# Where a softmax is divided by its sums: values normalised as they leave PSUM, or in the stage behind

## The chip, the cores and the metric

The kernel runs on one core of a Trainium2 chip. The metric is device time in microseconds (us) of a whole execution; lower is better. TensorE (PE in the profile) multiplies matrices into PSUM, VectorE (DVE) and ScalarE (ACT) read PSUM, GpSimd (POOL) works in SBUF, SyncE (SP) issues most transfers.

## The reference, cut to what matters

Two transformer layers with adaptive normalisation and experts. Only the first attention is touched: two softmaxes per head, whose difference is weighted with a number per head, lambda, and then normalised by its root mean square.

```python
lam = exp(sum(lambda_q1 * lambda_k1, -1)) - exp(sum(lambda_q2 * lambda_k2, -1)) + 0.8
A1, A2 = Q1 @ K1^T / sqrt(16), Q2 @ K2^T / sqrt(16)        # causal
attn = softmax(A1) - lam * softmax(A2)                     # B=2, H=16, N=2048
O = attn @ V                                               # 32 columns a head
O = O / sqrt(mean(O * O, -1) + 1e-5) * rms_scale * 0.2
x = x + gate * (O @ W_o^T)
```

## The kernel before, in words

`program` runs stages one after the other; a stage ends when all its engines have ended. `attention0` is the first attention, `attention0_out` (named `out0` in its buffers) the stage behind it.

**attention0** loops over 32 heads (batch times head). A head has 40 steps (`STEPS`), one for each pair of a query tile of 512 and a key block of 128 that the causal mask leaves; query tile 0 ends at step 3, tile 1 at 11, tile 2 at 23, tile 3 at 39 (`LAST`). Two steps make one iteration of TensorE. In an iteration TensorE computes four scores (L743, with the mask in L747) into a ring of three `ps_s`, ScalarE takes their exponentials into `probs` (L665), TensorE multiplies them with the values (L772) for both softmaxes at once, POOL adds the probabilities of the two steps (L635), and TensorE sums those over the keys with a matrix of ones (L783). Values and sums of a query tile lie in one `ps_o`, of which there are two: `[:, 0]` holds values, `[:, 1]` the sums, already repeated over the 32 rows of each value.

Between these matmuls TensorE slips in the *maxima* of a later head: 80 matmuls a head (L793) into a ring of three `ps_m`, of which VectorE takes the row maximum, with the mask (L691, two instructions) or without (L695). `maxima_at` spreads them: 42 in steps 20 to 39 for the head after the next one, and the other 38 in steps 0 to 17 for the next head. TensorE waits before each for `max_used`, that is until VectorE has read the maximum three before. After the 80th, VectorE reduces them (L699), TensorE turns them, VectorE splits them into three bf16 parts (L707 to L710) and SP writes those into the next head's `q_stack` (L598). For the first head all 80 of its own maxima come before its scores, and the next head's 80 are all in its steps 0 to 17.

When a query tile has ended, ScalarE copies values and sums, 512 columns, from `ps_o` to `results` (`take`, L650). `ends(k, 5)` puts that five steps after the tile's last step: before the exponentials of steps 8, 16 and 28 and of step 4 of the next head. It waits for the last ones matmul of the tile, and TensorE waits for `taken` before it starts the tile after next. SP then stores values (L613) and sums (L615), in two halves each, to `heads_out` and `exp_sums` in DRAM.

**attention0_out** works in 8 groups of 512 tokens, each in four tiles. SP loads `heads` and `total` of a group. TensorE turns the sums (L1048) and the heads (`turn`, L1056) so that tokens are rows. VectorE inverts the sums and weights the second one with lambda (L995, L997), multiplies (`normalise`, L1003), POOL subtracts (L951) and squares (L954), VectorE adds up the squares (L981). For the group before, meanwhile, `norm` takes L985, ScalarE's root, the reciprocal L987 and L990; TensorE turns back (L1063) and multiplies with W_o (L1086), and VectorE gates (L1011) and adds to x (L1014). In a step VectorE does `norm(now)`, the inversion, `normalise(after, 0)`, and then for each tile j `normalise(after, j + 1)`, `add(now, j)` and the squares of j. The stage begins with nine small loads (L903 to L907, four of them the lambdas) and the computation of lambda on VectorE and ScalarE.

The order around the takes, before:

```python
for k in range(N_STEPS):
    for a in range(2):
        ended = ends(k, 5)
        if a == 0 and ended and not (ended[1] and is_first(head)):
            take(head - 1 if ended[1] else head, ended[0])
```

## Time and profile before

| | us |
|---|---|
| three runs, median | 4081.42 (4077.68 to 4083.18) |
| the profiled execution, its own time | 4081.09 |
| its span, first to last instruction | 4079.1 |
| VectorE busy in the span | 2409.2 (59%) |
| ScalarE busy | 1599.8 (39%) |
| POOL busy | 1706.1 (42%) |

Durations come from the one profiled execution, whose time is 2.0 us above its span. In the list of groups a row gives line, engine, operation, output and input tiles, their shapes and the count; then the time in which the group was busy and the mean of one in ns; then how long the engine was idle just before and what ended that. In the order of time a row gives start and duration in us; several instructions of one kind may be merged into one row.

### The profile page before, as it was taken

Reading aid. Unit: us, or ns where it says so; the run is one execution under the profiler, and the core shown is the slowest. Engines: PE = TensorE matmul, PEld = TensorE weight load, DVE = VectorE, ACT = ScalarE, POOL = GpSimd, SP = SyncE. Lnnn points to the kernel's source line nnn. Section 1 sums busy time; section 2 is a strip of 40 time slices with the busy share of each in tenths; the row PEclk is TensorE's granted clock in tenths of the full one; section 3 lists DMA queues with packets and bytes.
Section 4 is the critical chain, followed back from the end, with each engine's and each line's share of the span. In section 5 each row is a group of like instructions: output and inputs, shape, how many; then the busy total and the mean of one; then the engine's idle time right before and its main releaser. Section 6 shows DMA issues by size and latency. Waiting matters only on the chain. (4 is left out here: it accounts for less than half of the span.)

```text
span 4079.1 us, 84288 instructions
## 1 busy us (share of the span) xinstructions
PE 3494.4 (86%) x27311; PEld 1870.2 (46%) x27311; DVE 2409.2 (59%) x5524; ACT 1599.8 (39%) x3266; POOL 1706.1 (42%) x1117
## 2 busy tenths in 40 slices
PE   6868999999999999999999967527999579895993
PEld 3322444444444444444444446524555345554562
DVE  3448777777777777777777347673111666666013
ACT  2322666666666666666666621101221321111110
POOL 1221665655656566656566644002443231110203
PEclk8987999999999999999999978557999789995997
DMA  4441111111111111111111031104332100001333
GB/s 156 145 141 41 35 42 43 35 46 42 34 46 36 41 42 35 47 36 41 44 35 46 11 119 65 43 0 119 78 80 52 43 15 0 1 0 50 115 113 93
DMA packets 229279, 224.88 MB, mean 55 GB/s; under 512 B 88722, under 2 KB 198547, under 8 KB 222739
## 3 DMA queue, kind: packets, MB, share of 16 engines
q1 hardware_dynamic: 213522, 194.33, 16.1%
q0 software_dynamic: 15360, 25.44, 3.2%
q8 instruction: 227, 3.72, 0.4%
q14 instruction: 170, 1.38, 0.1%
HBM read 138.58 MB, written 80.35 MB: 54 GB/s over the span
## 5 line engine op out<-in xcount | busy, mean ns | idle before, releaser
L635 POOL TENSOR_TENSOR attention_probs<-attention_probs 128x1024 f32<-128x1024 f32 (+2 forms) x640 | 1228.8, 1920 | 868.6 <-PE attention_ps_o L772 868.6
L665 ACT ACTIVATE attention_probs<-attention_ps_s 128x512 f32<-128x512 f32 (+3 forms) x2560 | 1197.7, 538 | 838.2 <-PE attention_ps_s L747 466.1
L695 DVE TENSOR_REDUCE attention_chunk_max<-attention_ps_m 128x1 f32<-128x512 f32 x1536 | 1005.5, 686 | 247.4 <-PE attention_ps_m L793 245.3
L793 PE MATMUL attention_ps_m<-attention_k_stack,attention_q_stack 96*128 96x512 bf16 (+3 forms) x2560 | 878.4, 358 | 43.2 <-DMA attention_v_head<-v_rows 33.9
L743 PE MATMUL attention_ps_s<-attention_q_stack,attention_k_stack 99*128 99x512 bf16 (+3 forms) x2560 | 798.5, 351 | 40.3 <-issue 27.2
L772 PE MATMUL attention_ps_o<-attention_probs,attention_v_head 128*32 128x256 f32 (+1 forms) x9728 | 640.5, 366 | 0.7 <-ACT attention_probs L665 0.4
L691 DVE CUSTOM_DVE_ANT_0 attention_ps_m<-attention_ps_m,attention_mask_wide 128x128 f32<-128x128 f32 (+3 forms) x1024 | 500.2, 498 | 219.3 <-PE attention_ps_m L793 201.7
L793 PEld LDWEIGHTS attention_ps_m<-attention_k_stack,attention_q_stack 96*128 96x128 bf16 x2560 | 243.6, 97 | 458.4 <-DVE attention_chunk_max L695 184.0
L783 PE MATMUL attention_ps_o<-attention_probs,consts 128*32 128x256 f32 (+1 forms) x5120 | 415.5, 360 | 0.4 <-POOL attention_probs L635 0.4
L772 PEld LDWEIGHTS attention_ps_o<-attention_probs,attention_v_head 128*32 128x32 f32 x9728 | 264.4, 109 | 273.6 <-issue 111.2
L743 PEld LDWEIGHTS attention_ps_s<-attention_q_stack,attention_k_stack 99*128 99x128 bf16 x2560 | 247.5, 98 | 306.1 <-ACT attention_probs L665 144.7
L783 PEld LDWEIGHTS attention_ps_o<-attention_probs,consts 128*32 128x32 f32 x5120 | 189.3, 110 | 89.5 <-POOL attention_probs L635 14.2
L747 PE MATMUL attention_ps_s<-mask_k_bf,ident_bf 128*128 128x128 bf16 x1024 | 221.4, 222 | 0.0
L1574 DVE TENSOR_TENSOR experts_hidT<-experts_ps_b,experts_silu 128x512 f32<-128x512 f32 x64 | 44.2, 691 | 238.4 <-ACT experts_silu L1540 238.4
L1521 POOL DMA_INDIRECT experts_sum<-experts_y_sb,experts_index x64 | 100.7, 1574 | 144.5 <-ACT experts_y_sb L1548 129.9
L379 POOL TENSOR_TENSOR project_parts<-project_rest,project_parts 128x512 bf16<-128x512 f32 x64 | 73.6, 1156 | 198.5 <-ACT project_parts L364 198.5
L2224 DVE TENSOR_SCALAR experts_hidT<-experts_ps_a 128x512 f32<-128x512 f32 x32 | 22.1, 691 | 212.3 <-PE experts_ps_a L2242 212.3
L691 DVE DVE_READ_ACCUMULATOR2_ANT attention_chunk_max<- 128x1 f32 x1024 | 144.9, 142 | 0.0
L1860 POOL TENSOR_TENSOR x<-x,linear_y 128x256 f32 (+1 forms) x32 | 24.6, 769 | 275.3 <-DVE linear_y L1918 275.3
L1957 PE MATMUL linear_ps_a<-linear_qblk,linear_kc 128*128 128x512 f32 x256 | 125.2, 616 | 3.2 <-POOL linear_vp L1856 2.7
L439 PE MATMUL project_ps_o<-project_hT,project_wqkv 128*128 128x512 f32 x256 | 113.4, 601 | 13.0 <-ACT project_hT L353 13.0
L1610 PE MATMUL experts_ps_y<-experts_w,experts_hidT 128*128 128x256 f32 x512 | 114.7, 382 | 10.4 <-DVE experts_hidT L1574 10.4
(278 smaller groups left out, 3935.2 us busy)
## 6 DMA issues: line engine op xcount, KB each, us to landing
qk_parts<-project_parts SPq DMA_DIRECT2D x64, 384.0 KB, 3.0
heads_out<-attention_results_sb SPq DMA_DIRECT2D x256, 64.0 KB
out_heads<-heads_out SPq DMA_DIRECT2D x8, 2048.0 KB, 7.9
experts_w<-in_f_w SPq DMA_DIRECT2D x16, 1024.0 KB, 8.4
attention_q_stack<-qk_parts SPq DMA_DIRECT2D x32, 384.0 KB
attention_k_stack<-qk_parts SPq DMA_DIRECT2D x32, 384.0 KB
experts_w<-in_e_w SPq DMA_DIRECT2D x24, 512.0 KB, 4.7
v_rows<-project_v SPq DMA_DIRECT2D x8, 1024.0 KB, 4.0
```

The source lines that it names most:

```text
L439: last = pe.matmul(ps_o[o % RING][:], w[:, o // 4, k, (o % 4) * P:(o % 4 + 1) * P], hT[:, k], start=(k == 0), stop=(k == DC - 1))
L635: pool.tensor_tensor(probs[:, to, :, lo:], probs[:, to, :, lo:], probs[:, k % RING_P, :, lo:], ALU.add).then_inc(pair_ok, 1)
L665: act.activation(probs[:, k % RING_P, a, left(k):], ps_s[(2 * k + a) % RING_S][:, left(k):], ACT.Exp, scale=float(DH) ** -0.5).then_inc(pr ...
L691: last = dve.tensor_tensor_reduce(ps_m[m % RING_M][:, 0:w], ps_m[m % RING_M][:, 0:w], mask_wide[:, GROUP - w:], 1.0, -3.0e38, ALU.add, ALU ...
L695: last = dve.tensor_reduce(to, ps_m[m % RING_M][:, 0:w], AX.X, ALU.max)
L743: last = pe.matmul(psum[:, lo:], ks[at][0:WITH_MAX, a, kb * P:(kb + 1) * P], qs[at][0:WITH_MAX, a, tq * GROUP + lo:(tq + 1) * GROUP], star ...
L747: last = pe.matmul(psum[:, lo:lo + P], core.ident_bf[:], core.mask_k_bf[:], start=False, stop=True)
L772: last = pe.matmul(psum[strip:strip + DV, 0, block:], vh[at][:, kb], halves(k, a, half, block), start=kb == 0, stop=False, tile_position=( ...
L783: last = pe.matmul(psum[strip:strip + DV, 1, block:], core.c("ones")[:, 0:DV], halves(k, a, half, block), start=False, stop=kb == GT * (tq ...
L793: pe.matmul(ps_m[m % RING_M][:, 0:w], qs[at][0:STACK, a, jq * P:(jq + 1) * P], ks[at][0:STACK, a, c * GROUP:c * GROUP + w], start=True, st ...
L1610: last = pe.matmul(ps_y[n][:, c], hT[:, m, (2 * n + c) * P:(2 * n + c + 1) * P], w_down[now.at][:, m], start=(m == 0), stop=(m == MC - 1))
L1957: last = pe.matmul(ps_a[hg][:, 4 * n:4 * n + 4].rearrange("p h t -> p (h t)"), kc[1 - at][:, hg], qblk[:, hg, 4 * n:4 * n + 4].rearrange(" ...
```

## The change

The division moves forward. In `attention0`, VectorE and no longer ScalarE takes a finished tile: a reciprocal of the 256 columns of sums from PSUM to SBUF, then one `scalar_tensor_tensor` that multiplies the 256 columns of values with a factor per partition and with the inverse. The factor is 1 on the partitions of the first softmax and minus lambda on those of the second. It is computed once, by VectorE and ScalarE, after the first head's maxima (`factors`), and its four loads are issued after the first head's. The take comes three steps after the tile's end (before the maxima of steps 6, 14, 26 and of step 2 of the next head). `results` has half its columns, and only values are stored. In `attention0_out` the totals, their transposes and their inversion go; ScalarE copies the second softmax's part from PSUM (`second`), VectorE adds the first one's to it (`difference`), and POOL only squares. The lambdas' loads and their computation are gone from the stage's start.

The diff, cut to its core:

```diff
@@ -44,7 +44,8 @@
...
                       ("iota", P), ("part", 1), ("headof", NE), ("blockdiag", NE * 17), ("tile_of", T * NE),
-                      ("expert", NE), ("expert_base", NE)):
+                      ("expert", NE), ("expert_base", NE),
+                      ("first_map", 1), ("second_map", 1)):
     CONSTS[_name] = (_at, _at + _width)
@@ -72,6 +73,8 @@
...
     put("expert_base", np.arange(NE)[None, :] * CAP1)
+    put("first_map", p // DV % 2 == 0)
+    put("second_map", -(p // DV % 2.0))
     return c
@@ -504,7 +507,11 @@
...
         probs = s.sb("probs", [P, RING_P, 2, GROUP], F32)
-        results = s.sb("results_sb", [P, RING_R, 2, BLOCKS, P], F32)
+        results = s.sb("results_sb", [P, RING_R, BLOCKS, P], F32)
+        inverse = s.sb("inverse_sb", [P, 2, BLOCKS, P], F32)
+        lam_in = s.sb("lam_in", [P, 4, H, DH], F32)
+        lam_two = s.sb("lam_two", [P, 2, H], F32)
+        factor = s.sb("factor", [P, B, H], F32)
         mask_wide = s.sb("mask_wide", [P, GROUP], F32)
@@ -583,6 +590,9 @@
...
                     load(after)
+                    for n, a in enumerate(lambdas):
+                        sp.dma_start(lam_in[:, n], a.rearrange("h d -> (h d)").partition_broadcast(P)
+                                     .rearrange("p (h d) -> p h d", h=H)).then_inc(lam_loaded, 16)
                 if later is not None:
@@ -611,10 +621,7 @@
...
                     sp.dma_start(oT[ds(h, 1), :, tile * GROUP:(tile + 1) * GROUP].rearrange(
-                        "n e (u v t) -> v (n e) u t", v=2, t=P)[half], results[rows, slot, 0]).then_inc(stored[slot], 16)
-                    sp.dma_start(sums[ds(h, 1), :, tile * GROUP:(tile + 1) * GROUP].rearrange(
-                        "n e (u v t) -> v (n e) u t", v=2, t=P)[half],
-                        results[half * 2 * DV:(half + 1) * 2 * DV:DV, slot, 1]).then_inc(stored[slot], 16)
+                        "n e (u v t) -> v (n e) u t", v=2, t=P)[half], results[rows, slot]).then_inc(stored[slot], 16)
@@ -640,14 +647,8 @@
...
-            act.sem_inc(taken, RING_O)
-            def take(head, turn):
-                slot = turn % RING_R
-                act.wait_ge(stored[slot], (head * (Q_TILES // RING_R) + 1) * (STORES * 16))
-                act.wait_ge(values_ok, head * N_STEPS + LAST[turn] + 1)
-                act.wait_ge(ones_ok, head * PAIRS + (LAST[turn] + 1) // PAIR + RING_P // PAIR)
-                act.activation(results[:, slot], ps_o[turn % RING_O][:], ACT.Copy).then_inc(taken, 1)
+            act.wait_ge(lam_steps, 3)
+            act.activation(lam_two[:], lam_two[:], ACT.Exp).then_inc(lam_exp, 1)
@@ -655,17 +656,12 @@
...
                     for a in range(2):
-                        ended = ends(k, 5)
-                        if a == 0 and ended and not (ended[1] and is_first(head)):
-                            take(head - 1 if ended[1] else head, ended[0])
                         act.wait_ge(score_ok, head * 2 * N_STEPS + 2 * k + a + 1)
...
                                        ACT.Exp, scale=float(DH) ** -0.5).then_inc(prob_ok, 1)
-                if after is None:
-                    take(head, Q_TILES - 1)
@@ -680,7 +676,34 @@
             dve.sem_inc(max_used, RING_M)
+            dve.sem_inc(taken, RING_O)
             dve.wait_ge(ready, 1)
+            def factors():
+                link = Counted(dve, lam_steps)
+                dve.wait_ge(lam_loaded, 4 * 16)
+                link.then(dve.tensor_tensor(lam_in[:, 0], lam_in[:, 0], lam_in[:, 1], ALU.mult))
+                link.then(dve.tensor_tensor(lam_in[:, 2], lam_in[:, 2], lam_in[:, 3], ALU.mult))
+                dve.tensor_reduce(lam_two[:, 0], lam_in[:, 0], AX.X, ALU.add)
+                link.then(dve.tensor_reduce(lam_two[:, 1], lam_in[:, 2], AX.X, ALU.add))
+                dve.wait_ge(lam_exp, 1)
+                link.then(dve.tensor_tensor(factor[:, 0], lam_two[:, 0], lam_two[:, 1], ALU.subtract))
+                link.then(dve.tensor_scalar(factor[:, 0], factor[:, 0], LAMBDA_INIT, core.c("second_map"), ALU.add,
+                                            ALU.mult))
+                link.then(dve.tensor_scalar(factor[:, 0], factor[:, 0], core.c("first_map"), None, ALU.add))
+                link.then(dve.tensor_copy(factor[:, 1], factor[:, 0]))
+            def take(head, turn):
+                psum, slot = ps_o[turn % RING_O], turn % RING_R
+                wait_apart(dve, values_ok, head * N_STEPS + LAST[turn] + 1, core.passed)
+                dve.wait_ge(ones_ok, head * PAIRS + (LAST[turn] + 1) // PAIR + RING_P // PAIR)
+                dve.reciprocal(inverse[:, turn % 2], psum[:, 1]).then_inc(inverted, 1)
+                wait_apart(dve, stored[slot], (head * (Q_TILES // RING_R) + 1) * (STORES * 16), core.passed)
+                dve.wait_ge(inverted, head * Q_TILES + turn + 1)
+                dve.scalar_tensor_tensor(results[:, slot], psum[:, 0],
+                                         factor[:].rearrange("p b h -> p (b h)")[:, ds(head, 1)],
+                                         inverse[:, turn % 2], ALU.mult, ALU.mult).then_inc(taken, 1)
@@ -714,11 +737,17 @@
...
                     maxima(next_head.n, range(len(MAXIMA)))
+                    factors()
                     return
                 for k in range(N_STEPS):
+                    ended = ends(k, 3)
+                    if ended and not (ended[1] and is_first(at_head.n)):
+                        take(at_head.n - 1 if ended[1] else at_head.n, ended[0])
                     whose, items = maxima_at(at_head.n, k, next_head, later)
...
                         maxima(whose.n, items)
+                if next_head is None:
+                    take(at_head.n, Q_TILES - 1)
@@ -913,31 +933,35 @@
...
                     "(r n) e t -> (n e) r t", n=2)).then_inc(loaded[at], 16)
-                sp.dma_start(total[at][:], sums[b * H:(b + 1) * H, :, ds(start, GROUP)].rearrange(
-                    "n e t -> (n e) t")).then_inc(loaded[at], 16)
...
                         step(b, i * 2 + (b * NG + at), i, at)
-            sp.wait_ge(loaded[0], B * NG * 16)
-            sp.wait_ge(loaded[1], B * NG * 16)
+            sp.wait_ge(loaded[0], B * NG // 2 * 16)
+            sp.wait_ge(loaded[1], B * NG // 2 * 16)
...
         def _(act):
-            act.wait_ge(lam_prod, 1)
-            act.activation(lam_two[:], lam_two[:], ACT.Exp).then_inc(lam_exp, 1)
+            def second(after, j):
+                act.wait_ge(turned_h, after * GT + j + 2 + GT)
+                act.wait_ge(sum_ok, after * GT + j + 1)
+                act.activation(two[:, j % 2], ps_h[j % 2][:, :, 1], ACT.Copy).then_inc(two_ok, 1)
             def step(now, after, at, pair):
-                if now is None:
-                    return
-                act.wait_ge(mean_ok, now + 1)
-                act.activation(mean[at][:], mean[at][:], ACT.Sqrt).then_inc(root_ok, 1)
+                if now is not None:
+                    act.wait_ge(mean_ok, now + 1)
+                    act.activation(mean[at][:], mean[at][:], ACT.Sqrt).then_inc(root_ok, 1)
+                if after is not None:
+                    second(after, 0)
                 for j in range(GT):
-                    act.wait_ge(y_ok, now * GT + j + 1)
-                    act.wait_ge(turned_o, now * GT + j + 1)
-                    act.activation(oT_sb[:, j % 2], ps_t[:], ACT.Copy).then_inc(oT_ok, 1)
+                    if after is not None and j + 1 < GT:
+                        second(after, j + 1)
+                    if now is not None:
+                        act.wait_ge(y_ok, now * GT + j + 1)
+                        act.wait_ge(turned_o, now * GT + j + 1)
+                        act.activation(oT_sb[:, j % 2], ps_t[:], ACT.Copy).then_inc(oT_ok, 1)
@@ -947,33 +971,22 @@
...
                 for j in range(GT):
-                    pool.wait_ge(two_ok, after * GT + j + 3)
-                    pool.tensor_tensor(o[1 - at][:, j], two[:, j, :, 0], two[:, j, :, 1], ALU.subtract)\
-                        .then_inc(sub_ok, 1)
-                    pool.wait_ge(sub_ok, after * GT + j + 1)
+                    pool.wait_ge(sum_ok, after * GT + j + 3)
                     pool.tensor_tensor(square[:, j], o[1 - at][:, j], o[1 - at][:, j], ALU.mult).then_inc(square_ok, 1)
         def _(dve):
-            chain = Counted(dve, lam_ok)
-            dve.wait_ge(w_in, 16 * 9)
-            chain.then(dve.tensor_tensor(lam_in[:, 0], lam_in[:, 0], lam_in[:, 1], ALU.mult))
-            chain.then(dve.tensor_tensor(lam_in[:, 2], lam_in[:, 2], lam_in[:, 3], ALU.mult))
-            dve.tensor_reduce(lam_two[:, 0], lam_in[:, 0], AX.X, ALU.add)
-            dve.tensor_reduce(lam_two[:, 1], lam_in[:, 2], AX.X, ALU.add).then_inc(lam_prod, 1)
-            dve.wait_ge(lam_exp, 1)
-            chain.then(dve.tensor_tensor(lam[:], lam_two[:, 0], lam_two[:, 1], ALU.subtract))
-            chain.then(dve.tensor_scalar(lam[:], lam[:], LAMBDA_INIT, None, ALU.add))
+            chain = Counted(dve, gate_ok)
+            dve.wait_ge(w_in, 16 * 5)
             dve.tensor_scalar(w[:].rearrange("p k n -> p (k n)"), w[:].rearrange("p k n -> p (k n)"), scale[:, 0:1],
...
-            dve.sem_inc(two_ok, 2)
+            dve.sem_inc(sum_ok, 2)
             dve.sem_inc(x_ok, 4)
@@ -990,20 +1003,9 @@
...
-            def invert_totals(after):
-                dve.wait_ge(turned_l, after + 1)
-                dve.reciprocal(recip[:], ps_l[:]).then_inc(l_steps, 1)
-                dve.wait_ge(l_steps, 2 * after + 1)
-                dve.tensor_tensor(recip[:, :, :, 1], recip[:, :, :, 1],
-                                  lam[:].unsqueeze(1).broadcast_to([P, GT, H]), ALU.mult).then_inc(l_steps, 1)
-                dve.wait_ge(l_steps, 2 * after + 2)
-            def normalise(after, j):
-                dve.wait_ge(turned_h, after * GT + j + 2 + GT)
-                dve.tensor_tensor(two[:, j].rearrange("p h a d -> p (h a) d"),
-                                  ps_h[j % 2][:].rearrange("p h a d -> p (h a) d"),
-                                  recip[:, j].rearrange("p h a -> p (h a)").unsqueeze(2)
-                                  .broadcast_to([P, 2 * H, DV]), ALU.mult).then_inc(two_ok, 1)
+            def difference(after, j, at):
+                dve.wait_ge(two_ok, after * GT + j + 1)
+                dve.tensor_tensor(o[at][:, j], ps_h[j % 2][:, :, 0], two[:, j % 2], ALU.add).then_inc(sum_ok, 1)
@@ -1018,12 +1020,11 @@
...
                 if after is not None:
-                    invert_totals(after)
-                    normalise(after, 0)
+                    difference(after, 0, 1 - at)
                 for j in range(GT):
                     if after is not None and j + 1 < GT:
-                        normalise(after, j + 1)
+                        difference(after, j + 1, 1 - at)
                     if now is not None:
@@ -1040,18 +1041,9 @@
-            def turn_totals(after, place, pair):
-                wait_apart(pe, loaded[place], pair * 32 + 32, core.passed)
-                for j in range(GT):
-                    last = pe.matmul(ps_l[:, j].rearrange("p h a -> p (h a)"), total[place][:, j * P:(j + 1) * P],
-                                     core.c("ident")[0:2 * H, 0:2 * H], start=True, stop=True)
-                last.then_inc(turned_l, 1)
             def turn(after, place, j):
-                pe.wait_ge(two_ok, after * GT + j + 1)
+                pe.wait_ge(sum_ok, after * GT + j + 1)
                 for r in range(ROWS):
@@ -1066,7 +1058,7 @@
                 if after is not None:
-                    turn_totals(after, 1 - at, pair + at)
+                    wait_apart(pe, loaded[1 - at], (pair + at) * 16 + 16, core.passed)
                     turn(after, 1 - at, 0)
```

## Rows read from the trace of the kernel before

**Rows 1.** Stretch: us; PE, PEld, DVE, ACT, POOL busy; PEclk, DMA share, GB/s

```profile
380.00:2373.00 1993.00, 1949.84 (x20793) 908.48 (x20791) 1422.60 (x3581) 1237.73 (x2667) 1221.77 (x637) 0.99 0.15 38
```

**Rows 2.** Instructions of the line that ends each head's maxima

```profile
L699 DVE TENSOR_REDUCE attention_neg_max<-attention_chunk_max x32: 285/286/289, 352.1 to 2289.5; 128x32 f32<-128x128 f32 x32
```

**Rows 3.** Instruction groups by form: busy us, mean ns, idle before

```profile
L650 ACT ACTIVATE attention_results_sb<-attention_ps_o 128x512 f32<-128x512 f32 x128 | 75.9, 593 | 2.1 <-PE attention_ps_o L783 2.1
L987 DVE RECIPROCAL out_mean_sq<-out_mean_sq 128x64 f32<-128x64 f32 x8 | 4.4, 553 | 2.6 <-ACT out_mean_sq L935 2.6
L995 DVE RECIPROCAL out_recip<-out_ps_l 128x128 f32<-128x128 f32 x8 | 7.6, 950 | 4.5 <-PE out_ps_l L1048 4.5
L1189 DVE SCALAR_TENSOR_TENSOR gates_h<-gates_scaled,gates_rstd,rows 128x256 f32<-128x256 f32 x64 | 26.8, 480 | 3.4 <-DVE gates_scaled L1182 3.4
```

**Rows 4.** VectorE in order of time, in one head: start us, duration us

```profile
1236.73 1.28 DVE L695 TENSOR_REDUCE attention_chunk_max<-attention_ps_m 128x1 f32<-128x512 f32 x2
...
1261.50 0.69 DVE L695 TENSOR_REDUCE attention_chunk_max<-attention_ps_m 128x1 f32<-128x512 f32 x1
...
1267.42 0.29 DVE L691 CUSTOM_DVE_ANT_0 attention_ps_m<-attention_ps_m,attention_mask_wide 128x128 f32<-128x128 f32 x1
...
1279.90 0.42 DVE L691 CUSTOM_DVE_ANT_0 attention_ps_m<-attention_ps_m,attention_mask_wide 128x256 f32<-128x256 f32 x1
1280.24 0.69 DVE L695 TENSOR_REDUCE attention_chunk_max<-attention_ps_m 128x1 f32<-128x512 f32 x1
1281.96 1.29 DVE L695 TENSOR_REDUCE attention_chunk_max<-attention_ps_m 128x1 f32<-128x512 f32 x2 [1.03 <-PE attention_ps_m L793]
```

**Rows 5.** TensorE in the same stretches

```profile
1238.65 0.38 PE L793 MATMUL attention_ps_m<-attention_k_stack,attention_q_stack 96*128 96x512 bf16 x1
...
1263.18 0.33 PE L793 MATMUL attention_ps_m<-attention_k_stack,attention_q_stack 96*128 96x384 bf16 x1
...
1270.39 0.38 PE L793 MATMUL attention_ps_m<-attention_k_stack,attention_q_stack 96*128 96x512 bf16 x1
...
1281.98 0.38 PE L793 MATMUL attention_ps_m<-attention_k_stack,attention_q_stack 96*128 96x512 bf16 x1
...
1283.06 0.38 PE L793 MATMUL attention_ps_m<-attention_k_stack,attention_q_stack 96*128 96x512 bf16 x1
```

**Rows 6.** Order of time, VectorE after the first head's maxima

```profile
360.59 0.30 DVE L691 CUSTOM_DVE_ANT_0 attention_ps_m<-attention_ps_m,attention_mask_wide 128x128 f32<-128x128 f32 x1 [6.47 <-PE attention_ps_m L793]
```

**Rows 7.** One line of the stage behind, once a group

```profile
L985 DVE TENSOR_SCALAR out_mean_sq<-out_mean_sq x8: 194/195/196, 2406.8 to 2554.7; 128x64 f32<-128x64 f32 x8
```

**Rows 8.** Order of time in the stage behind, VectorE and POOL

```profile
2445.18 0.41 DVE L1011 TENSOR_TENSOR out_gated<-out_ps_y,out_gate 128x256 f32<-128x256 f32 x1
2445.34 1.26 POOL L951 TENSOR_TENSOR out_o<-out_two 128x512 f32<-128x512 f32 x1 [0.91 <-DVE out_two L1003]
2445.74 1.14 DVE L1014 TENSOR_TENSOR x<-x,out_gated 128x256 f32 x1
...
2452.53 0.95 DVE L995 RECIPROCAL out_recip<-out_ps_l 128x128 f32<-128x128 f32 x1
...
2453.86 1.23 DVE L1003 TENSOR_TENSOR out_two<-out_ps_h,out_recip 128x1024 f32<-128x1024 f32 x1
```

**Rows 9.** A group by form: an addition-like instruction of PSUM and SBUF

```profile
L1574 DVE TENSOR_TENSOR experts_hidT<-experts_ps_b,experts_silu 128x512 f32<-128x512 f32 x64 | 44.2, 691 | 238.4 <-ACT experts_silu L1540 238.4
```

**Rows 10.** Order of time, start of the stage behind

```profile
2376.87 0.37 SPq L903 DMA_DIRECT2D out_lam_in<-in_lq  x1
...
2378.71 0.43 SPq L905 DMA_DIRECT2D out_wo<-in_wo  x1
...
2391.48 1.88 PE L1048 MATMUL out_ps_l<-consts,out_total 32*128 32x32 f32 x8 [20.93 <-DMA out_total<-exp_sums]
```

**Rows 11.** Stretches again, for the granted clock (columns as in rows 1)

```profile
1005.00:1006.00 1.00, 0.72 (x5) 0.50 (x6) 0.00 (x0) 0.08 (x1) 0.00 (x0) 0.50 0.63 188
...
2425.00:2430.00 5.00, 3.04 (x25) 2.69 (x24) 4.47 (x9) 0.26 (x1) 1.90 (x2) 1.00 0.36 128
```

More of the change, by code:

```diff
@@ L487, in __init__, with attention0 @@
         self.n, self.at, self.round = STACKS * i + n, n % STACKS, i + n // STACKS
-def attention0(nc, core, qk_parts, v_rows, oT, sums):
+def attention0(nc, core, qk_parts, v_rows, oT, lambdas):
     with stage(nc, "attention0") as s:
@@ L524, in attention0 @@
         PAIRS = N_STEPS // PAIR
[L525 removed]
+        STORES = 2
         LAST = [k for k, (_, tq, kb) in enumerate(STEPS) if kb == GT * (tq + 1) - 1]
@@ L868, in attention0_out @@
         heads = [s.sb(f"heads{i}", [P, 2 * DQ // P, GROUP], F32) for i in range(2)]
-        total = [s.sb(f"total{i}", [2 * H, GROUP], F32) for i in range(2)]
-        recip = s.sb("recip", [P, GT, H, 2], F32)
-        two = s.sb("two", [P, GT, H, 2, DV], F32)
+        two = s.sb("two", [P, 2, H, DV], F32)
         o = [s.sb(f"o{i}", [P, GT, H, DV], F32) for i in range(2)]
@@ L901, in _ @@
         def _(sp):
-            for n, a in enumerate(lambdas):
-                sp.dma_start(lam_in[:, n], a.rearrange("h d -> (h d)").partition_broadcast(P)
-                             .rearrange("p (h d) -> p h d", h=H)).then_inc(w_in, 16)
             sp.dma_start(w[:], woT.rearrange("(k p) n -> p k n", p=P)).then_inc(w_in, 16)
```

24 lines of the change are left out of this document (9 added, 15 removed).

## The prediction

> **What bounds the kernel now.** I read the stage windows first, to see which engine fills the first attention. There TensorE is busy 1949.84 of 1993 us, VectorE 1422.60, ScalarE 1237.73, at a granted clock of 0.99, that is 2.4 GHz [rows 1]. In VectorE's order of time the pauses end with TensorE's matmuls L793, as the 1.03 us before 1281.96 [rows 4]: it has idle time and TensorE has none. The line that closes each head's maxima (L699) starts 32 times, from 352.1 to 2289.5 us, so a head takes 62.5 us on average [rows 2]. Whatever holds TensorE there counts in full, 32 times over; whatever VectorE gets counts only where its idle time and the three ps_m buffers don't cover it. The stage behind alternates: VectorE works alone on norm and totals while TensorE waits, then both work.
>
> **What leaves ScalarE.** 128 copies of 0.593 us, 75.9 us in all [rows 3]. ScalarE idles 755 us of the stage and TensorE's iterations with such a copy are no longer than those without, so I take 0; in the last one and a half heads, where no maxima fill TensorE, five copies may be worth up to 0.5 us each: -1 us of the -2.5 to 0.
>
> **What comes to VectorE.** 128 takes: a reciprocal of 256 columns out of PSUM and a scalar_tensor_tensor of 256 columns. Reciprocals of 64 and 128 columns took 553 and 950 ns [rows 3]: 6.2 ns a column, so 950 + 128 x 6.2 = 1744 ns for 256. The nearest scalar_tensor_tensor took 480 ns [rows 3], and its successor can start some 80 ns before its end, as successive maxima do (1279.90 + 0.42 against 1280.24 [rows 4]). With 0.04 us for the wait between the two, a take holds VectorE for 1.74 + 0.04 + 0.40 = 2.18 us. The Trainium skill ("VectorE: DVE Perf Modes", First, the fixed hardware budget) states that Reciprocal is an iterative divide with a repeat count of 8; at the page's 0.96 GHz that would be 8.3 ns a column, an estimate of 2.0 us for 256 and a sum some 33 us higher. The rows show 6.2 ns, and the sum goes by them.
>
> Where does it hit? VectorE meets a take before the maxima of steps 2, 6, 14 and 26 of the 40. The ones matmuls that it needs are over by then, since TensorE has already issued the maxima of the two steps before, so the take itself waits for nothing. But the next maximum starts 2.18 us later, and TensorE may be only three maxima ahead. For step 14 of one head: VectorE would start the next maximum not at 1279.90 but at 1282.08 and end it at 1282.50 [rows 4]. TensorE's matmul of 1281.98 writes that buffer again [rows 5]; with 0.05 us for the semaphore it starts at 1282.55, 0.57 late. The next maxima follow at 1282.42 and 1283.02 and the third ends at 1283.71; the matmul of 1283.06, late by 0.57, is held until 1283.76: 0.70 us lost. VectorE then catches up in the 1.03 us in which it idled [rows 4]. In the same way step 2 (VectorE 1261.50, TensorE's matmul of 1263.18): 1261.50 + 2.18 + 0.69 + 0.05 = 1264.42, 1.24 late. Step 26 (1236.73 and 1238.65): 1239.65, 1.00 late. Step 6 (1267.42 and 1270.39): the maxima of 0.21 and 0.60 go first, the third ends at 1271.10, so 1271.15, 0.76 late [rows 4, 5]. Together 3.70 us a head. TensorE has nothing to catch up with, so they stay.
>
> 30 takes of each of the four kinds fall beside maxima: 30 x 3.70 = 111 us. The two of the first head fall where 80 maxima are crowded into 18 steps and VectorE is nearly the bound: 2 us each, 4 us. The other six have no maxima behind them; the last one ends the stage with 2.18 instead of 0.59 us, and two DMA issues of L615 drop out, an estimated 0.6 us each: +0.4 us. Waits that could replace it: values of the turn after next need the buffer that a take frees; the nearest is step 2, over at 1261.50 + 2.18 = 1263.68, and needed by values that follow two more maxima behind the matmul of 1263.18 [rows 5], still in time. SP's stores come two steps earlier, half as many. The lambdas' chain, eight small instructions and one of ScalarE, falls into the gap of 6.47 us in which VectorE waits before the second head's maxima [rows 6]: 0, and if the chain did not fit, 3 us at most. **Attention: +114 us**, bounds +66 (each take 0.4 us cheaper, as small gaps ahead of TensorE's values absorb some) and +155 (0.3 us dearer, if register work ahead of each wait shows, and 4 more).
>
> **The stage behind.** The eight L985 start from 2406.8 to 2554.7, 21.1 us apart [rows 7]. After norm, VectorE inverts the totals from 2452.53 to 2453.86 and then normalises in 1.22 us, after which TensorE may go on [rows 8]. That becomes one addition of PSUM and SBUF of 512 columns, 0.69 us as L1574 [rows 9]; ScalarE copies its part (about 0.59 us, as L650 [rows 3]) while VectorE norms. Saved: 1.33 + 0.53 = 1.86 us. Behind it VectorE has two more normalisations on its path: 2 x 0.53 = 1.06. So 2.9 us in each of 7 cycles: 20.3 us. At the start: four lambda loads issued before the rest, 2376.87 to 2378.71, 1.84 us; the transposed totals, 1.88 us [rows 10]; 1.3 us in the first tile (copy and addition for normalisation and POOL's difference), and about 0.8 us in each of three tiles whose pace POOL sets, with 1.26 us for the difference [rows 8] ahead of the square: 7.4 us. **Stage behind: -28 us**, bounds -38 (the shorter pause leaves TensorE at 2.4 GHz) and -10 (only the inversion counts).
>
> Sum: 111 + 4 - 1 + 0.4 - 27.7 = +87 us, on the profiled execution's own 4081.09 us, which is 0.3 us below the median of the three runs: 4168 us.
>
> **The rivals.**
> *Absorbed, so faster.* The takes would vanish in VectorE's idle time. Idle time is enough on average (570 us against 279), which speaks for it; against it, the idle pieces are about 1 us long and a take 2.18. The lost 3.70 us a head are 4 x 2.18 less a cover of 5.0, 1.25 us a take, so net zero needs 0.22 us lost, a take of about 1.5 us. That wants a reciprocal nearer to 1 us; the rows would have to bend. With no loss at all it gives 4081 - 28 = 4053 us. Chance of landing below -0.2%: 0.06, and 0.03 between.
> *POOL's sums block the new instruction.* An addition with both inputs in SBUF (L1014) took 1.14 us while POOL's L951 ran, though it is as wide as L1011 just before it; L1011, with one input in PSUM, kept its 0.41 beside the same POOL instruction [rows 8]. The new instruction has one tensor in PSUM, one in SBUF and a pointer scalar in SBUF. If it is held like L1014, POOL's sums, busy 1221.77 of 1993 us [rows 1], cost 0.61 x about 1.1 = 0.7 us a take: + 85, 4253 us. 0.07. The Trainium skill ("SBUF — State Buffer", Who interferes with whom) states that VectorE with two SBUF inputs contends with a GpSimd instruction that reads SBUF, and with one at most it does not; whether the scalar counts decides this rival. For plain tensors the rows agree.
> *The clock falls.* After a pause of 3.7 us in TensorE the granted clock was 0.50, that is 1.2 GHz [rows 11]. If each 1 us hole did that for some 5 us, half of it lost, 122 x 2.5 = 305: 4473 us. Against it: 3.04 busy of 5 us left it at 1.00 [rows 11]. 0.03. The Trainium skill ("TensorE: Matmul & The Clock Gate", A second HAM failure mode) tells of a kernel where short idles between groups made the clock oscillate; by it this rival would be the forecast.
> *No cover at all.* VectorE the bound, each take in full: 122 x 2.18 - 28: 4319 us. 0.03.
>
> **The numbers.** Forecast 0.78; the rest as above. From the bounds: 4081 + 66 - 38 = 4109 and 4081 + 155 - 10 = 4226; widened by a us or two the range is 4108 to 4228, with the rivals outside it. What a measurement can tell here is about 0.2%, 8 us. Slower 0.91, same 0.03, faster 0.06.
>
> **What would show it.** Reciprocal rows near 1744 ns and the other near 480, x128; VectorE near 1700 us busy in the stage; heads 3.7 us longer each; TensorE's waits for VectorE grown by some 110 us, clock still 0.99; L985 about 18.2 us apart. Wrong if heads keep their length, or if scalar_tensor_tensor rows spread up to 2 us.

## The result and the profile after

The changed kernel takes 4175.53 us (median of 4 runs, 4173.57 to 4180.96) against 4082.30 us before: ratio 1.0231, 95% interval 1.0216 to 1.0245, so 93 us slower. The forecast was 4168, +87. The profiled execution took 4175.89 us, its span 4174.1; that is 95.0 us above the span before. By stages of the two traces: first attention (end of the first head's maxima to the issue of the last store, which before is one of the sums) 2148.7 against 2021.7 us, +127.0 (forecast +114); the stage behind it, to its last addition to x, 165.9 against 196.4, -30.5 (forecast -28); all else -1.5.

The page's first part, and the stretch that answers to [rows 1] (the attention now ends near 2500):

```profile
PE 3511.1 (84%) x27247; PEld 1863.0 (45%) x27247; DVE 2634.2 (63%) x5766; ACT 1572.2 (38%) x3170; POOL 1663.1 (40%) x1085
380.00:2500.00 2120.00, 1985.55 (x20815) 913.58 (x20807) 1678.07 (x3839) 1194.49 (x2541) 1222.69 (x637) 0.99 0.14 35
```

TensorE is busy for 94% of the stretch where it was 98%. Its idle time went from 43 to 134 us; its busy time too is 36 us longer, for as many matmuls. VectorE has 255 us more work and 442 us left idle. The granted clock is again 0.99. The two new groups, and the line that closes each head's maxima [rows 2], then the one of the stage behind [rows 7]:

```profile
L701 DVE RECIPROCAL attention_inverse_sb<-attention_ps_o 128x256 f32<-128x256 f32 x128 | 224.1, 1751 | 67.8 <-PE attention_ps_o L812 67.2
L704 DVE SCALAR_TENSOR_TENSOR attention_results_sb<-attention_ps_o,attention_factor,attention_inverse_sb 128x256 f32<-128x256 f32 x128 | 61.9, 484 | 8.0
L722 DVE TENSOR_REDUCE attention_neg_max<-attention_chunk_max x32: 285/286/289, 352.5 to 2416.4; 128x32 f32<-128x128 f32 x32
L998 DVE TENSOR_SCALAR out_mean_sq<-out_mean_sq x8: 194/194/195, 2525.2 to 2652.7; 128x64 f32<-128x64 f32 x8
```

The reciprocal took 1751 ns (forecast 1744), the multiplication 484 (480). A regular head, from one L722 to the next, is 65.0 to 65.2 us instead of 61.2: +3.9 (forecast 3.70). The groups of the stage behind stand (2652.7 - 2525.2) / 7 = 18.2 us apart, as forecast.

Step 14 of one head in order of time, VectorE and TensorE; it answers to [rows 4, 5], and it is the place that the prediction worked out:

```profile
1279.53 1.75 DVE L701 RECIPROCAL attention_inverse_sb<-attention_ps_o 128x256 f32<-128x256 f32 x1
1281.17 0.39 PE L822 MATMUL attention_ps_m<-attention_k_stack,attention_q_stack 96*128 96x512 bf16 x1
1281.32 0.48 DVE L704 SCALAR_TENSOR_TENSOR attention_results_sb<-attention_ps_o,attention_factor,attention_inverse_sb 128x256 f32<-128x256 f32 x1
1281.72 0.42 DVE L714 CUSTOM_DVE_ANT_0 attention_ps_m<-attention_ps_m,attention_mask_wide 128x256 f32<-128x256 f32 x1
1282.25 0.39 PE L822 MATMUL attention_ps_m<-attention_k_stack,attention_q_stack 96*128 96x512 bf16 x1 [0.48 <-DVE attention_chunk_max L714]
```

From the start of the take to the next maximum it is 1281.72 - 1279.53 = 2.19 us (forecast 2.18); then TensorE sits for 0.48 us until a maximum has freed its buffer. Summed over the stretch, the waits (us in total, times, longest; of the loading of weights, PEld, and of the matmuls, PE):

```profile
PEld attention_ps_m L822 <- DVE attention_chunk_max L718: 266.2, 587, 2.7
PEld attention_ps_m L822 <- DVE attention_chunk_max L714: 116.9, 254, 1.0
PE attention_ps_m L822 <- DVE attention_chunk_max L718: 60.3, 65, 2.4
PE attention_ps_m L822 <- DVE attention_chunk_max L714: 28.3, 64, 0.7
```

The second pair was 1.9 and 1.3 us before. It grew to 88.6 us over 129 waits: one real pause of the matmuls for each take. It is less than the 127.0 us lost. The ends of matmuls are modelled in this profile, so that part of each stall may stand in it as busy time, the 36 us above; that is argued and not shown.

The first head lost 7.5 us (64.2 against 56.7). In order of time, and the granted clock behind it (stretches, last three columns clock, DMA share, GB/s):

```profile
378.78 0.39 PE L822 MATMUL attention_ps_m<-attention_k_stack,attention_q_stack 96*128 96x512 bf16 x1 [2.39 <-DVE attention_chunk_max L718]
379.10 1.67 PE L801 MATMUL attention_ps_o<-attention_probs,attention_v_head 128*32 128x256 f32 x16
...
380.00:382.00 2.00, 2.00 (x18) 0.60 (x11) 0.13 (x1) 0.00 (x0) 1.13 (x1) 0.50 0.13 45
```

There the maxima are crowded, the pause was 2.39 us, and the clock fell to 0.50, that is 1.2 GHz: the 16 matmuls of values took 1.67 us, where they took 1.07 just before. The second take of that head did the same. After the pauses of the regular takes, 0.8 to 1.3 us, it did not fall.

### The profile page after: what moved, and what is told of

It is laid out like the page before. It is cut to its first block and busy times, and to the rows that moved or that the text cites. A ratio compares the mean times of both kernels' runs of the same rounds, so it can differ in the third digit from the quotient of the medians.

```text
span 4174.1 us, 83875 instructions
## 1 busy us (share of the span) xinstructions
PE 3511.1 (84%) x27247; PEld 1863.0 (45%) x27247; DVE 2634.2 (63%) x5766; ACT 1572.2 (38%) x3170; POOL 1663.1 (40%) x1085
## 5 line engine op out<-in xcount | busy, mean ns | idle before, releaser
L701 DVE RECIPROCAL attention_inverse_sb<-attention_ps_o 128x256 f32<-128x256 f32 x128 | 224.1, 1751 | 67.8 <-PE attention_ps_o L812 67.2
```

What stands on the lines that cost most here:

```text
L701: dve.reciprocal(inverse[:, turn % 2], psum[:, 1]).then_inc(inverted, 1)
```

## The experiments

The theory: TensorE has work in stock for about 1 to 1.5 us of VectorE's absence, the *cover*; what a take lasts beyond it is lost, and VectorE's idle total is of no account. Below, *excess* is how much longer an iteration of TensorE (two steps) is than in the first experiment, by the distance of ScalarE's exponentials four apart in the trace, as the median over heads. It is given for the take or piece that causes it; where the table of experiment 6 names steps, they are those of the exponentials, and what VectorE does at one step shows there two steps later.

**1. No reciprocal.** Take of 0.48 us; the division is left out, a constant 1 stands in its place.

```diff
+dve.memset(inverse[:], 1.0)
...
-dve.reciprocal(inverse[:, turn % 2], psum[:, 1]).then_inc(inverted, 1)
+dve.sem_inc(inverted, 1)
```

> The changed kernel without the attention's reciprocals: the values are multiplied by a constant 1 where the inverse of the sums stood, so the division is left out. Everything else, the wait for the sums at VectorE included, stands as in the changed kernel. Theory (the length of the take beyond what TensorE's stored work covers, 0.94 to 1.48 us by position, is what costs): a take of 0.48 us is covered at all four positions, a regular head falls from 65.0 to 61.2 us as before, the attention from 2148.7 to about 2022 us, and with the faster out stage (166 us) the total is about 4050 us. Rival (the wait for the sums at the front of VectorE's queue holds back the maxima, whatever the length of the take): the wait stays, so the heads stay between 63 and 65 us and the total lies between 4110 and 4175 us.

Measured: 4051.23 us (6 runs), ratio 0.993 (0.9909 to 0.9951). Regular head 61.1 to 61.2 us, attention 2026.6 (before: 2021.7), stage behind 166.1. The wait for the sums still stands in front of VectorE's queue and costs nothing in a regular head: there the length of the reciprocal is the whole loss. The attention is still 4.9 us longer than before: 1.5 us in the first head, 4.6 us in the eight heads in which the loop turns (one in three), less 1.1 us behind the last maxima. This kernel has no reciprocal, so none of that is the reciprocal's.

**2. ScalarE takes the values alone.** VectorE takes nothing; division and lambda are left out.

```diff
+act.activation(results[:, slot], ps_o[turn % RING_O][:, 0], ACT.Copy).then_inc(taken, 1)
```

> ScalarE takes the turns as in the kernel before and at its place, but only the 256 columns of the values; VectorE takes nothing. The division and the weighting with lambda are left out; the out stage is the changed one. Theory: ScalarE's copies of half the size cost TensorE nothing, a regular head is 61.2 us, the attention is within 2 us of 2021 us, the out stage 166 us, and the total about 4050 us, within 5 us of the kernel without reciprocals. Rival (taking the copies off ScalarE was worth something that the gain of the kernel without reciprocals includes): the heads here are 0.3 to 1 us longer than in that kernel, and the total is 10 to 30 us above it.

Measured: 4054.06 us (4 runs), ratio 0.9934 (0.9909 to 0.9959); regular head 61.2, attention 2027.1. That ScalarE is relieved is worth nothing that can be seen, as the prediction had it. Both kernels show about what the new stage behind is worth: -29 to -32 us by the medians.

**3. More beyond the cover.** A second reciprocal of 256 columns, and in another kernel one of 128, written to a tile that nobody reads.

```diff
+dve.reciprocal(again[:], psum[:, 1])
 dve.reciprocal(inverse[:, turn % 2], psum[:, 1]).then_inc(inverted, 1)
```

> The changed kernel with each of the attention's reciprocals run twice, the first into a tile that nobody reads. Theory (the cover is used up, so that each further microsecond of VectorE at a take is a microsecond of TensorE): 1.75 us more a take, the four iterations of a head with a take lengthen by 2.5 to 3.0 us over before, a head is 72 us, and the total is 4175.5 + 128 x 1.75 = about 4400 us. Rival (pauses of TensorE as long as the 2.39 us one of the first head halve the granted clock each time): each take costs 2 to 3 us more again, a head is 80 us or more, and the total is 4650 us or more, with granted clock 0.50 behind each take. Second rival (VectorE has 570 us of idle time in the steady stretch before and takes up work without loss): less than 4300 us.

> The changed kernel with a further reciprocal of 128 columns at each take, into a tile that nobody reads: half of what the kernel with two reciprocals adds. It gives a point between pauses of TensorE of 1 us, behind which the granted clock stayed at 1.00, and the 2.4 us pause of the first head, behind which it fell to 0.50. Theory (linear while the clock holds): 0.95 us more a take, 3.8 us a head, 69 us a head, total 4175.5 + 128 x 0.95 = about 4297 us, and the granted clock stays at 1.00 in regular heads. Rival (the clock already falls at pauses near 2 us): some heads 71 us and more with stretches at 0.50, total 4330 us or more.

Measured: 4533.34 us with 256 columns more, between the theory's 4400 and the rival's 4650; 4346.10 with 128 more, where the theory gave 4297 and its rival, that the clock falls, 4330 or more: there the rival holds (two runs each). In stretches of clock 1.00 the theory is nearly right: at step 14 the excess went from 0.65 us to 1.46 (of 0.95 us added) and 2.26 (of 1.75 added), 0.85 to 0.92 us for each microsecond. The rest is the clock. The smaller dose, TensorE in order of time and the stretches from 966 us:

```profile
966.12 0.34 PE L824 MATMUL attention_ps_m<-attention_k_stack,attention_q_stack 96*128 96x384 bf16 x1 [1.89 <-DVE attention_chunk_max L720]
966.29 0.85 PE L774 MATMUL attention_ps_s<-attention_q_stack,attention_k_stack 99*128 99x512 bf16 x2
966.94 0.63 PE L824 MATMUL attention_ps_m<-attention_k_stack,attention_q_stack 96*128 96x512 bf16 x1
...
966.00:970.00 4.00, 3.88 (x25) 1.51 (x28) 2.99 (x9) 1.68 (x3) 0.00 (x0) 0.57 0.19 63
970.00:973.00 3.00, 3.00 (x39) 1.54 (x35) 2.26 (x4) 2.04 (x4) 2.35 (x1) 1.00 0.19 71
```

The matmul that took 0.39 us takes 0.63. Such a fall made an iteration 4.91 us instead of 3.33, so 1.6 us each, and came one, two or three times a head (heads of 69.7, 71.3 and 72.8 us; with none, an estimate from these, it would be about 68.2); over 380 to 2350 us the granted clock was 0.95, with the full second reciprocal 0.91. Pauses of 1.2 to 2.7 us were followed by a fall at some times and not at others.

**4. The take at another place.** The same take two steps later.

```diff
-ended = ends(k, 3)
+ended = ends(k, 5)
```

> The changed kernel with each whole take five steps behind the turn's end, where ScalarE took it before, and not three. Nothing else differs. Theory (TensorE's cover differs by position, and at step 4 it is the bank itself that TensorE waits for): the turns 0, 1 and 2 cost 0.7 to 1.3 us each, turn 3 about 3.4 us, 1.3 of maxima and 2 of waiting for its bank at the next head's turn 1; a regular head is 66.5 to 67.5 us and the total 4220 to 4260 us. Rival (the place is of no account, only the length is): 65 us a head and 4175 us.

Measured: 4274.25 us (2 runs), above both the theory's 4260 and the rival's 4175. A regular head is 68.0 to 68.7 us in twenty cases and 66.5, as the theory had it, in two. In these two the excess by take is 2.0 us for the one at step 4, 1.26 at step 8, 1.11 at step 16 and 0.97 at step 28. So the place counts. At step 4 it is the bank of the turn after next that is not free; in the waits of TensorE, from 380 us:

```profile
PE attention_ps_o L801 <- DVE attention_results_sb L704: 55.0, 28, 2.0
```

That is 1.96 us in each of 28 heads, a wait that the changed kernel does not have. It stands in place of the stall for the maxima there and is not added to it, as the expectation had it (1.3 and 2).

The other 1.6 us of a head are the clock again. In 27 of the 30 heads with maxima it fell behind this very pause. The matmuls behind it in two heads one after the other, and the stretches (the last three columns are clock, DMA share, GB/s):

```profile
533.57 1.07 PE L801 MATMUL attention_ps_o<-attention_probs,attention_v_head 128*32 128x256 f32 x16 [1.93 <-DVE attention_results_sb L704]
600.10 1.94 PE L801 MATMUL attention_ps_o<-attention_probs,attention_v_head 128*32 128x256 f32 x16 [1.93 <-DVE attention_results_sb L704]
...
533.50:536.50 3.00, 2.94 (x35) 1.55 (x35) 2.56 (x7) 1.07 (x3) 1.75 (x1) 1.00 0.19 66
600.00:603.00 3.00, 2.90 (x26) 1.27 (x27) 1.31 (x4) 0.00 (x0) 0.85 (x1) 0.51 0.19 66
```

Both pauses are 1.93 us; behind the first the clock stays at 1.00 and the 16 matmuls take 1.07 us, behind the second it is 0.51 and they take 1.94. Of the 3.1 us by which a head of 68.1 is longer than the changed kernel's 65.0, the place has 1.5 and the clock 1.6.

**5. The take in pieces.** The whole computation; the reciprocal in two halves, at iterations of their own.

```diff
+dve.reciprocal(inverse[:, turn % 2, u], psum[:, 1, u]).then_inc(inverted, 1)   # u = 0, 1
...
+OFFSETS = ((3, 3, 3, 3), (5, 5, 5, 5), (5, 5, 5, 5))    # halves: steps behind the end, by turn
+OFFSETS = ((3, 3, 3, 3), (5, 5, 5, 3), (7, 7, 7, 3))    # thirds
```

> The whole computation of the changed kernel, with the take in two parts: the reciprocal of the first 128 columns of the sums at three steps behind the turn's end (0.95 us by the row of that size), the one of the other 128 and the multiplication two steps later (0.95 + 0.48 us). VectorE's work is the same plus 0.15 us a take. Theory (a cover for each iteration, 0.94 to 1.48 us): the first part is hidden everywhere, the second exceeds the cover by 0 to 0.5 us at a take; a regular head is 61.2 to 63 us and the total 4050 to 4110 us, 4070 the likeliest. Rival (the cover is a stock that is used up once and is not filled again two steps later, or it is VectorE's total that counts): the heads stay at 65 us or above and the total at 4175 us or above.

> The whole computation, the take in three parts for turns 0, 1 and 2: the reciprocal of the first 128 columns of the sums three steps behind the turn's end, the one of the other 128 five steps, the multiplication seven steps behind; the turn 3 is taken whole at three steps behind, as in the changed kernel. Theory (a piece of up to about 1 us is covered and the cover is full again two steps later, and the take in halves lost most of what it lost because TensorE waited at the turn 1's first values for the turn 3's bank, 82 us, 2.2 us a head of 63.4): the turns 0, 1 and 2 cost nothing, turn 3 costs its 1.3 us as in the changed kernel, a regular head is 62.5 us, the total 4050 + 32 x 1.3 = about 4092 us. Rival (the sum of VectorE's work near a turn's end counts, however it is cut): 63.4 us or more a head and 4132 us or more, since a further instruction is added.

Halves: 4132.40 us, ratio 1.0129 (1.0101 to 1.0157), regular head 63.4: below the rival's 4175, but above the theory's 4110 and 63 us. Thirds: 4102.87 us, 1.0045 (1.0029 to 1.0061), 62.5. So the cover is there anew at each iteration: the first halves of 0.95 us cost 0 everywhere, though VectorE's work grew. The second part of 1.43 us cost 0.46, 0.31 and 0.17 us at steps 8, 16 and 28, and 1.28 us at step 4. The expectation for the thirds put 2.2 us a head on that last wait; this added PEld's and PE's waits, which lie mostly in the same time, and PE's alone are 1.24 us each, near the 1.28 of the excess (the waits of the halves' kernel):

```profile
PEld attention_ps_o L819 <- DVE attention_results_sb L708: 44.9, 27, 1.7
PE attention_ps_o L819 <- DVE attention_results_sb L708: 37.1, 30, 1.3
```

That bank wait is what the halves' expectation had left out. The thirds' head of 62.5 us was right: turns 0, 1 and 2 at 0, turn 3, still taken whole at step 2, at 1.23. The total was forecast as 4092, 11 us too low; the regular heads are not where that was missed.

**6. ScalarE empties PSUM, VectorE divides the copy.** Full computation. ScalarE copies 512 columns at five steps as before; VectorE's pieces follow from SBUF, where no bank waits for them.

```diff
+act.activation(raw[:, turn % 2], ps_o[turn % RING_O][:], ACT.Copy).then_inc(taken, 1)
...
+dve.reciprocal(inverse[:, turn % 2, u], raw[:, turn % 2, 1, u]).then_inc(inverted, 1)
...
+OFFSETS = ((9, 7, 7, 7), (11, 9, 9, 9), (11, 11, 11, 11))
```

> The whole computation with another division of the work: ScalarE copies values and sums out of PSUM at five steps behind a turn's end, as in the kernel before, and VectorE inverts the copy in SBUF in two halves and multiplies, seven to eleven steps behind the turn's end, each piece at an iteration of its own where that can be. The out stage is the changed one. Theory (pieces of up to 1 us are covered, and no bank waits for VectorE): a regular head is 61.2 to 61.8 us, the attention 2022 to 2045 us and the total 4050 to 4072 us, below the kernel before by 0.3 to 0.8%. Rival (the multiplication, now with both tensors in SBUF, is held back by GpSimd's sums or slows them): the multiplication takes over 1 us, some heads are 63 us, and the total is 4100 us or more. Rival (VectorE's 570 us of idle time are in truth TensorE's slack, and 2.4 us a take cannot be hidden anywhere): 65 us a head and 4175 us.

Measured: 4099.13 us (12 runs, one of them 4158.01), ratio 1.0033 (1.0022 to 1.0044): better than the change, not better than before, and above the 4050 to 4072 us of the theory. Regular head 62.4. Nearly all of the excess lay in one iteration, 1.16 us at step 22 of the exponentials; VectorE and TensorE there:

```profile
1058.42 1.76 DVE L714 RECIPROCAL attention_inverse_sb<-attention_raw 128x128 f32<-128x128 f32 x2 [0.32 <-DVE attention_max_parts L762]
...
1060.49 0.39 PE L852 MATMUL attention_ps_m<-attention_k_stack,attention_q_stack 96*128 96x512 bf16 x1 [1.06 <-DVE attention_chunk_max L743]
```

Between steps 18 and 20 VectorE has no maxima, so two pieces that were meant for two iterations ran as one of 1.76 us, just before the later head's maxima began. Three kernels moved turn 1's pieces on, nothing else:

```diff
-OFFSETS = ((9, 7, 7, 7), (11, 9, 9, 9), (11, 11, 11, 11))
+OFFSETS = ((9, 7, 7, 7), (11, 11, 9, 9), (11, 13, 11, 11))    # steps 18, 22, 24
+OFFSETS = ((9, 7, 7, 7), (11, 15, 9, 9), (11, 17, 11, 11))    # steps 18, 26, 28
+OFFSETS = ((9, 13, 7, 7), (11, 15, 9, 9), (11, 17, 11, 11))   # steps 24, 26, 28
```

> The kernel with ScalarE's copies and VectorE's pieces behind them, with one place changed: of turn 1, the second reciprocal is moved from step 20 to step 22 and the multiplication from step 22 to step 24. In that kernel the two reciprocals of turn 1 ran back to back, since VectorE has no maxima between steps 18 and 20, and the iteration at step 20, where the later head's maxima begin, was 1.16 us longer in each head, the whole excess of a regular head (62.4 against 61.2 us). Theory (that one place is the cost): a regular head is 61.2 to 61.4 us, the attention 2025 to 2040 us, and the total 4099 - 31 x 1.16 = about 4063 us, below the kernel before by 0.3 to 0.6%. Rival (the excess comes from VectorE's larger total, and appears elsewhere when it is taken away here): a regular head stays at 62.2 us or above and the total at 4090 us or above.

> The same again, with turn 1's second reciprocal at step 26 and its multiplication at step 28, where no other piece lies. With them at steps 22 and 24 a regular head was 61.7 us: 0.34 us of excess stood at step 22 and 0.12 us at step 24. Theory (these two places, just behind the point where the later head's maxima begin, have less cover than the others; elsewhere a piece of 0.95 us is free): a regular head is 61.2 to 61.3 us and the total 4077.5 - 31 x 0.46 = about 4063 us, below the kernel before by 0.3 to 0.7%. Rival (what is left comes from the total of VectorE's work): a regular head stays at 61.7 us, with the excess at another step, and the total at 4077 us.

> The same again, with turn 1's first reciprocal moved as well, from step 18 to step 24; the second stays at step 26 and the multiplication at step 28. After the last move 0.35 us of excess stood at step 22 in each head though no piece lay between steps 18 and 26, so that only the reciprocal at step 18, which runs behind the chain that ends the head's maxima, could be late there. Theory (that reciprocal delays the later head's first maxima): the iteration at step 22 is 2.93 us again, a regular head 61.2 to 61.3 us and the total 4073.8 - 31 x 0.35 = about 4063 us. Rival (another cause, such as the longer wait of the stores in SyncE's queue): step 22 stays at 3.28 us and the total at 4074 us. A third outcome: a new excess of 0.1 to 0.4 us appears at step 24, next to the place where a multiplication had cost 0.12 us, and the total is 4065 to 4074 us.

| turn 1's pieces at steps | us | ratio to before, 95% | regular head | excess at the exponentials of 22, of 24 |
|---|---|---|---|---|
| 18, 20, 22 | 4099.13 | 1.0033 (1.0022 to 1.0044) | 62.4 | 1.16, 0 |
| 18, 22, 24 | 4077.50 | 0.9987 (0.9977 to 0.9996) | 61.7 | 0.34, 0.12 |
| 18, 26, 28 | 4073.77 | 0.9979 (0.9967 to 0.9991) | 61.6 | 0.35, 0 |
| 24, 26, 28 | 4061.48 | 0.9952 (0.9939 to 0.9966) | 61.3 | 0, 0 |

The first of the moves fell short of its theory, and the second refuted what I had made of the rest: the excess at 22 stayed though the second reciprocal had gone to step 26. It came from the reciprocal at step 18. With that one moved too, the last kernel computes all that the changed one does and takes 114 us less, and 21 us less than the kernel before. Its stretch, which holds for the whole steady part of the attention:

```profile
380.00:2300.00 1920.00, 1883.63 (x19978) 882.93 (x19976) 1682.13 (x3945) 1183.89 (x2550) 1169.47 (x608) 0.99 0.15 39
L751 DVE TENSOR_REDUCE attention_neg_max<-attention_chunk_max x32: 285/286/290, 351.1 to 2294.7; 128x32 f32<-128x128 f32 x32
```

VectorE is busy for 88% here, more than the 79% of the changed kernel, and a regular head is 61.3 us against 61.2 without the division: the same work, cut and placed. What it gains over the kernel before is the stage behind (166.0 against 196.4 us); its attention is 2029.2 us against 2021.7, 4.1 us of that in the first head.

## Why the prediction came out right

*What bounds the kernel.* Right. TensorE's lost time is the cost, VectorE's 442 us of idle time do not help; experiments 1 and 3 show both sides of the cover, and the last kernel shows that it is length and place, not the total. The total came within 8 us in part by luck: the attention cost 13 us more than forecast, and the stage behind and all else gave 4 us of it back.

*Price of the take.* 2.18 us forecast, 2.19 measured. The Trainium skill ("VectorE: DVE Perf Modes", First, the fixed hardware budget) states that Reciprocal is an iterative divide with a repeat count of 8; the estimate made from that count (950 ns for the first 128 columns, the count for the others) was 2.0 us for 256. The row shows 1.751, and 6.3 ns for each column from 128 (948 ns) to 256: the measurement decides against reading that count as eight cycles a column.

*Stall a head.* 3.70 us forecast (1.24, 0.76, 0.70, 1.00 at steps 2, 6, 14, 26). Excess over experiment 1: 1.22, 0.88, 0.72, 1.01, together 3.83. The walk through one head's order of time, buffer by buffer, was good to 0.15 us. The term of 111 us for 30 heads was in truth 119. Against experiment 1 the same heads grew by 114.5 us, 3.82 each, so the takes account for 4 us of the difference. The other 4.6 us are not the reciprocal's: experiment 1 has them too, in the eight heads where the loop turns, and why is not shown.

*First head.* The term that was mis-sized most: 4 us forecast, 7.5 measured. The pauses were 2.39 us where 2 were forecast, and the clock fell behind them, shown above; and 1.5 us stand there with the short take of experiment 1 as well. The rival *the clock falls* was dismissed for the regular heads, where it stayed away, and holds in the one head where the pause was twice as long. Experiments 3 and 4 give it its price, 1.6 us a fall. The Trainium skill ("TensorE: Matmul & The Clock Gate", A second HAM failure mode) tells of short idles that make the clock oscillate; the changed kernel's regular takes, with pauses of 0.8 to 1.3 us, do not do that, the kernels of experiments 3 and 4, with pauses up to 2.7 us, do.

*ScalarE's relief.* 0 in regular heads, right (experiment 2). The +0.4 at the end came, the -1 did not: from the last head's maxima to the last store it is 84.8 us against 84.3. In experiments 1 and 2 that stretch is 83.2 and 83.0 us, 1.1 and 1.3 below before, which is about what the two store issues of L615 that are no longer there took (0.53 us each). So no run shows a gain from ScalarE's relief there.

*Lambda chain.* Hidden, right: VectorE still waited 3.25 us behind it for TensorE, where it had waited 6.47 [rows 6].

*Stage behind.* -30.5 against -27.7. The cycles gave 20.4 us (forecast 20.3), the start 8.9 (7.4), the last group 1.2 that I had not counted. Experiments 1 and 2 found the same stage at 166.1 and 168.2 us.

*The rivals.* Absorbed: it would have needed a take under about 1 us; cut in such pieces it is absorbed, which is the last kernel (4061 us, with 4053 given for no loss at all). No cover: refuted by the pieces at 0. GpSimd's sums block the multiplication: refuted for this operand pattern (484 ns at most 486, with 98 of 128 under a sum of GpSimd's), and true for the other, below.

## What to carry to other kernels

Idle time of an engine in percent says nothing on what it can take up; ask for how long the bounding engine can go on without it at that place, and walk through the order of time with the new instruction in it. An instruction that is longer than this stock costs its overhang each time, however idle the engine is on average, and a long pause can cost the clock as well (experiments 3 and 4): cut it, give each piece an iteration of its own, and see that two pieces don't meet in a gap and run as one. Where a consumer holds a buffer that the bounding engine needs, let an engine with a short instruction empty it, and do the slow work on the copy.

## What was not expected of the hardware

The same `scalar_tensor_tensor`, with its tensor from SBUF and not from PSUM, is held by GpSimd. In experiment 6 the group has a mean of 661 ns; counted in the order of time, 62 of 128 with no sum of GpSimd's beside them took 473 to 486 ns, 66 beside one took up to 1887, median 1057:

```profile
L720 DVE SCALAR_TENSOR_TENSOR attention_results_sb<-attention_raw,attention_factor,attention_inverse_sb 128x256 f32<-128x256 f32 x128 | 84.6, 661 | 3.9
...
1010.35 2.35 POOL L643 TENSOR_TENSOR attention_probs<-attention_probs 128x1024 f32<-128x1024 f32 x1 [0.92 <-PE attention_ps_o L831]
1011.93 1.06 DVE L720 SCALAR_TENSOR_TENSOR attention_results_sb<-attention_raw,attention_factor,attention_inverse_sb 128x256 f32<-128x256 f32 x1
...
1042.49 0.48 DVE L720 SCALAR_TENSOR_TENSOR attention_results_sb<-attention_raw,attention_factor,attention_inverse_sb 128x256 f32<-128x256 f32 x1
```

The instruction at 1011.93 waited out GpSimd's sum, which ends at 1012.70, and went on to 1012.99. The Trainium skill ("SBUF — State Buffer", Who interferes with whom) has it so for two SBUF inputs against one; both sides agree with these rows. The instruction that reads PSUM, one SBUF tensor and a scalar per partition in SBUF stayed at 482 to 486 ns in all 128 cases, so here the scalar did not count as the second input. That the other one was held cost nothing, in a piece with cover to spare.

A reciprocal of 128 columns took 938 ns from SBUF and 948 from PSUM: the source makes no difference to it.

What stays open: what decides whether the clock falls behind a pause of 1.2 to 2.7 us (two of 1.93 us went both ways); and whether the last kernel's 10 us over experiment 1 by the medians are a cost, since the two profiled spans, 4055.0 and 4053.0 us, are only 2 us apart.
